# A convolution with per-image mixed weights on one core: the first image pair's five input transfers on two DMA queues, and small products moved around them

## The chip, the core and the metric

The kernel runs on one core of one Trainium2 chip. A core has five engines with instruction streams of their own: TensorE (PE, matrix products into PSUM), VectorE (DVE), ScalarE (ACT), GpSimd (POOL) and SyncE (SP, here only DMA issues and waits). SyncE and ScalarE each ask for DMA transfers on a hardware queue of their own; the profile calls them q1 and q10. Sixteen DMA engines move the data of both. The metric is the device time in microseconds, 304.93 us as the median of three runs of the kernel before (304.77 to 305.39).

## The reference

For x of shape (32, 64, 56, 56), with K = 4 sets of 3x3 weights:

```python
g = gn(x)                                     # group norm, 32 groups of 2 channels, over 2 x 56 x 56 values
pooled = g.mean(axis=(2, 3))
a = relu(einsum('bc,kc->bk', pooled, fc1_w) + fc1_b)
att = softmax(einsum('bk,jk->bj', a, fc2_w) + fc2_b, axis=1)
agg_w = einsum('bk,koihw->boihw', att, weight)     # weights of 64 x 64 x 3 x 3 for each image
agg_b = att @ bias
out = x + conv(g, agg_w, padding=1) + agg_b
```

So an image's convolution can't start before its whole input has been read: the statistics give the attention, the attention mixes the four weight sets, and the mixed weights are what TensorE multiplies with.

## The kernel before

Two images make a pair: 16 pairs, with image and channel on the 128 partitions (2 x 64) and 3136 pixels along a row. All is float32 in memory. For the products, inputs and weights are scaled and split in a high and a low float16 part (xh, xl and wh, wl), and each output tile sums three kinds of product: high by high, high inputs by low weights, low inputs by high weights. Each kind has nine taps, on two 64 x 64 halves of the array. This is the line L1063, 6912 recorded products, in the function `products`.

The order of each engine's instructions is written out by hand, one function for each engine, and semaphores tie them together. Pairs 1 to 15 are prepared while TensorE works on the pair before. Pair 0 has nothing to hide behind, and all that this change touches is its preparation, in this order:

- SyncE (L313 to L323) asks for x0 in four pieces (`PIECES`, in chunks of 448 pixels: 0-2, 2-4, 4-5, 5-7), each with a semaphore `x_piece`. When piece 0 has landed it asks for the first two weight sets, when the last piece has landed for the other two, and when the first half of the weights is there for pair 1's four quarters.
- ScalarE (L916) asks for `small`, the tensor with the attention's weights and biases, then loads its table. It sums chunk 2 of x0 by itself (`sum_chunk`, L882), and after the statistics squares the first two weight sets (`squares`, L874).
- VectorE (`first_stats`, L443) takes the statistics of the other six chunks of 448 pixels, then aggregates them (L472 to L495), forms the logits (L552 to L556) and in `first_mixture` (L631 to L642) the diagonals of the attention and the first third of the mixed weights.
- GpSimd works on b1_part from `small` (L380), then on the moments of chunk 2 (L401 to L410), then the two roots rstd and wnorms (L414, L417), and eye_exsum (L421).
- TensorE runs constant products on ones (`keep_warm`, L1043; their numbers are `WARM_PRODUCTS`), whose results nobody reads, between the small products that it is needed for: the sums (L1010), the range of values (`first_range`, L1016 to L1021), and `part_sum` (L1031, L1037), two shares of the mixed weights. Its first convolution product waits for wh, which ScalarE makes (L863) from VectorE's mix (L642).

Of the kernel before, what the change touches and what calls it, by code (L numbers as in the profile page):

```python
# [28 lines left out]
CHUNK = 448  # L29
CHUNKS = PIX // CHUNK  # L30

PIECES = ((0, 2), (2, 4), (4, 5), (5, 7))
PIECE_OF = (0, 0, 1, 1, 2, 3, 3)

GATE = 0

# [18 lines left out]
TURNED = (2, 3, 0, 1)  # L55

X_RING = 4
WARM_PRODUCTS = (38, 8, 12, 6, 3, 3)

EARLY = 4  # L60

# [48 lines left out]
def dynamic_conv(nc, x, w_t, small, out):  # L110
# [7 lines left out]
    with ctx:  # L118
# [6 lines left out]
        def sem(name):  # L125
            return ctx.enter_context(nc.semaphore(name))
# [86 lines left out]
        s_eye = sem("s_eye")  # L213
        s_diagonal = sem("s_diagonal")
        s_exsum = sem("s_exsum")
        s_eye_exsum = sem("s_eye_exsum")
        s_part_sum = sem("s_part_sum")
        s_const = sem("s_const")
# [57 lines left out]
        def lower_rows(p, m, g, groups=1):  # L276
# [2 lines left out]
            rows *= groups  # L279
            return out_d[p][halves[m], row * W:(row + rows) * W], o_sb[p % 2][1][halves[1 - m], at:at + rows * W]  # L280

        block = ctx.enter_context(nc.Block())

        @block.sync
        def _(sp):
            def load_quarter(p, n):
                if p >= X_RING:

                    for half in range(2):
                        sp.wait_ge(s_xl[half], p - X_RING + 1)  # L290
                pixels = slice(n * HALF // 2, (n + 1) * HALF // 2)
                sp.dma_start(x_sb[p % X_RING][:, pixels], x_d[p, :, pixels]).then_inc(x_in[p % X_RING][n % 2], 16)

            def quarter_landed(p, n):

                sp.wait_ge(x_in[p % X_RING][n % 2], 32 * (p // X_RING - (p % X_RING == 0)) + 16 * (n // 2 + 1))

            def cross_params(p):
                i = p % 2
                sp.wait_ge(s_par, p + 1)  # L300
                for m in range(2):
                    sp.dma_start(crossed[i][halves[1 - m], :], par[i][halves[m], :]).then_inc(s_outp[i], 16)

            def store_groups(p, g, groups=1):

                i, n = p % 2, GROUPS * p + g + groups - 1
                sp.wait_ge(s_res, 2 * n + 1)
                sp.dma_start(*upper_rows(p, g, groups)).then_inc(stored[i][0], 16)
                sp.wait_ge(s_res, 2 * n + 2)
                for m in range(2):  # L310
                    sp.dma_start(*lower_rows(p, m, g, groups)).then_inc(stored[i][1], 16)

            for n, (first, end) in enumerate(PIECES):  # L313
                pixels = slice(first * CHUNK, end * CHUNK)
                sp.dma_start(x_sb[0][:, pixels], x_d[0, :, pixels]).then_inc(x_piece[n], 16)  # L315

            for n, (piece, ks) in enumerate(((GATE, slice(0, 2)), (len(PIECES) - 1, slice(2, K)))):
                sp.wait_ge(x_piece[piece], 16)
                sp.dma_start(w_sb[:, ks, :], w_t[:, ks, :]).then_inc(s_weights[n], 16)
            sp.wait_ge(s_weights[0], 16)  # L320
            for n in range(4):
                load_quarter(1, n)
            cross_params(0)  # L323

            for p in range(2, X_RING):
                for n in range(4):
                    if n >= 2:
                        quarter_landed(p, n - 2)
                    else:
                        quarter_landed(p - 1, n + 2)  # L330
                    load_quarter(p, n)
            for p in range(GROUPED):

                store_groups(p, 0, SLOTS)
                cross_params(p + 1)
                load_quarter(p + X_RING, 0)
                store_groups(p, SLOTS)
                for n in range(1, 4):
                    if n >= 2:
                        quarter_landed(p + X_RING, n - 2)  # L340
                    load_quarter(p + X_RING, n)
            for p in range(GROUPED, PAIRS):

                for g in range(GROUPS if p < last_pair else GROUPS - 1):
                    store_groups(p, g)
                    if g == 2 and p < last_pair:
                        cross_params(p + 1)
                    if p + X_RING < PAIRS:
                        load_quarter(p + X_RING, g)
            i, g = last_pair % 2, GROUPS - 1  # L350
            sp.wait_ge(s_res, 2 * GROUPS * PAIRS - 1)
            sp.dma_start(*upper_rows(last_pair, g)).then_inc(stored[i][0], 16)
            sp.wait_ge(s_res_last, 1)
            sp.dma_start(*lower_rows(last_pair, 0, g)).then_inc(stored[i][1], 16)
            for i in range(2):
                for r in range(2):
                    sp.wait_ge(stored[i][r], 16 * (1 + r) * transfers(PAIRS + i))
# [68 lines left out]
        def _(dve):  # L426
# [146 lines left out]
            def first_scale_step(k):  # L573

                if k == 0:
                    dve.wait_ge(s_exsum, 1)
                    nc.vector.reciprocal(rsum[:], exsum[:]).then_inc(dch, 1)
                    dve.wait_ge(s_range, 3)
                    nc.vector.reciprocal(rtotal[:], total).then_inc(dch, 1)
                elif k == 1:  # L580
                    dve.wait_ge(dch, 4)
# [42 lines left out]
            def first_mixture():  # L624

                dve.wait_ge(s_exp, 1)
                part = PARTS[0]
                dve.wait_ge(s_const, 3)

                for k in range(SUMMED_SHARES):  # L630
                    nc.vector.tensor_scalar(diagonals[:, k, :], eye[:], ex[:, k:k + 1], None, ALU.mult).then_inc(s_diagonal, 1)  # L631
                nc.vector.tensor_reduce(exsum[:], ex[:], AX.X, ALU.add).then_inc(s_exsum, 1)
                dve.wait_ge(s_weights[1], 16)
                nc.vector.tensor_scalar(part_mix[:], w_sb[:, 2, part], ex[:, 2:3], None, ALU.mult).then_inc(s_part, 1)
                first_scale_step(0)
# [44 lines left out]

            def weights_bound():

                dve.wait_ge(s_range, 3)
                nc.vector.tensor_scalar(wbound[:], tiny[1][:, WEIGHTS:WEIGHTS + 1], 1.0 / C, None,
                                        ALU.mult).then_inc(s_bound, 1)

            def low_weights(p):
# [107 lines left out]
        def _(act):  # L795
# [101 lines left out]
            def results(p, g, regions=range(2)):  # L897
                i, n = p % 2, GROUPS * p + g
                for r in regions:
                    if g == 0:  # L900
# [7 lines left out]
                        if p >= 2:  # L908
# [4 lines left out]
                    nc.scalar.activation(o_sb[i][r][:, at:at + rows * W], acc[n % SLOTS][r][:, 0:rows * W], ACT.Identity,  # L913
                                         bias=scales[:, 1:2], scale=scales[:, 0:1]).then_inc(s_res, 1)

            act.dma_start(small_sb[:], small).then_inc(s_small, 16)  # L916
            act.wait_ge(s_warm, 1)
            nc.scalar.activation(warm[:], warm[:], ACT.Exp)
# [78 lines left out]
        def _(pe):  # L997
# [14 lines left out]

            def first_range():

                pe.wait_ge(s_wnorms, 1)
                nc.tensor.matmul(tiny[1][:, WEIGHTS:WEIGHTS + 1], scale[:], wnorms[:],  # L1016
                                 start=True, stop=True).then_inc(s_range, 1)
                nc.tensor.matmul(tiny[1][:, RANGE:RANGE + 1], scale[:], wnorms[:], start=True, stop=False)
                pe.wait_ge(s_first_std, 1)
                for m in range(2):  # L1020
                    nc.tensor.matmul(tiny[1][halves[m], RANGE:RANGE + 1], ones[halves[m], 0:C], std[0][halves[m], :],  # L1021
                                     start=False, stop=True).then_inc(s_range, 1)

            def part_sum():

# [70 lines left out]
            first_range()  # L1096
            keep_warm(3)
            part_sum()
            keep_warm(4)

            pe.wait_ge(s_part, 2)
# [126 lines left out]
```

## Time and profile before

| | |
|---|---|
| median of 3 runs | 304.93 us (304.77 to 305.39) |
| profiled execution, its own time | 304.70 us |
| its span | 302.9 us |
| TensorE busy | 297.3 us (98%) |
| VectorE, ScalarE, GpSimd busy | 246.0, 189.8, 17.7 us |
| chain of waits, share of TensorE | 95% |
| first convolution product | 14.26 us |
| granted TensorE clock | 0.998 |

The span runs from the first to the last recorded instruction; the execution's own time is longer. Times in the rows are microseconds from the span's start. In the chain of waits each piece is what the next one waited for, so only a change in a piece of the chain, or one that puts something else in its place, moves the end.

### The profile page before, as it was taken

Reading aid. Unit: us, or ns where it says so; the run is one execution under the profiler, and the core shown is the slowest. Engines: PE = TensorE matmul, PEld = TensorE weight load, DVE = VectorE, ACT = ScalarE, POOL = GpSimd, SP = SyncE. Lnnn points to the kernel's source line nnn. Section 1 sums busy time; section 2 is a strip of 40 time slices with the busy share of each in tenths; the row PEclk is TensorE's granted clock in tenths of the full one; section 3 lists DMA queues with packets and bytes.
Section 4 is the critical chain, followed back from the end, with each engine's and each line's share of the span. In section 5 each row is a group of like instructions: output and inputs, shape, how many; then the busy total and the mean of one; then the engine's idle time right before and its main releaser. Section 6 shows DMA issues by size and latency. Waiting matters only on the chain.

```text
span 302.9 us, 15877 instructions
## 1 busy us (share of the span) xinstructions
PE 297.3 (98%) x7066; PEld 273.2 (90%) x7066; DVE 246.0 (81%) x799; ACT 189.8 (63%) x246; POOL 17.7 (6%) x30
## 2 busy tenths in 40 slices
PE   8899999999999999999999999999999999999995
PEld 6678997799978997799999999999999999999874
DVE  3898998989999999998998989699696978956000
ACT  3766739194683927385496869567685866768222
POOL 2221040402100000000000000000000000000000
PEclk9999999999999999999999999999999999999999
DMA  7957875737547575846808898685758342332333
GB/s 266 307 166 191 284 231 161 218 131 197 161 150 224 161 208 173 225 157 170 239 26 236 243 232 276 155 257 164 209 135 235 96 122 70 111 101 80 95 112 104
DMA packets 26868, 53.62 MB, mean 177 GB/s; under 512 B 6064, under 2 KB 16432, under 8 KB 26800
## 3 DMA queue, kind: packets, MB, share of 16 engines
q1 hardware_dynamic: 26576, 52.53, 58.6%
q8 instruction: 55, 0.90, 1.3%
q14 instruction: 13, 0.11, 0.1%
q10 hardware_dynamic: 224, 0.07, 0.1%
HBM read 26.89 MB, written 25.69 MB: 174 GB/s over the span
## 4 chain that ended last, share of the span: by engine, by line
PE 95%; DMA 2%; DVE 1%; SPq 0%; issue 0%; POOL 0%; ACT 0%; DVEq 0%
PE acc L1063 94%; DMA x<-x 2%; SPq L315 0%; DVE stats L443 0%; PE tiny L1004 0%; PE acc L1031 0%; PE acc L1043 0%; POOL rstd L414 0%; DVE mv L478 0%; DVE o L791 0%; ACT wh L863 0%; PE tiny L1016 0%; DVE mix L642 0%; PE tiny L1010 0%; DVE sums L490 0%
## 5 line engine op out<-in xcount | busy, mean ns | idle before, releaser
L1063 PE MATMUL acc<-xh,wh 64*64 64x385 f16 (+5 forms) x2304 | 112.6, 325 | 0.3 <-ACT wh L863 0.3
L1063 PE MATMUL acc<-xh,wl 64*64 64x385 f16 (+5 forms) x2304 | 112.4, 325 | 0.0
L1063 PE MATMUL acc<-xl,wh 64*64 64x385 f16 (+5 forms) x2304 | 111.7, 325 | 0.0
L1063 PEld LDWEIGHTS acc<-xl,wh 64*64 64x64 f16 x2304 | 91.4, 107 | 5.9
L1063 PEld LDWEIGHTS acc<-xh,wl 64*64 64x64 f16 x2304 | 90.6, 107 | 6.7
L1063 PEld LDWEIGHTS acc<-xh,wh 64*64 64x64 f16 x2304 | 89.6, 107 | 7.4 <-ACT wh L863 0.5
L913 ACT ACTIVATE o<-acc,par 128x392 f32<-128x392 f32 (+1 forms) x64 | 43.0, 672 | 56.8 <-PE acc L1063 56.8
L457 DVE BATCH_NORM_STATS2 stats<-x 128x6 f32<-128x448 f32 x105 | 61.2, 618 | 1.9
L834 ACT ACTIVATE xh<-x,xof,xsc 128x1568 f16<-128x1568 f32 x24 | 40.5, 1692 | 25.2 <-DVE xof L544 24.7
L701 DVE TENSOR_TENSOR xl<-x,xh 128x1568 f16<-128x1568 f32 x28 | 49.8, 1783 | 3.4 <-ACT x L801 3.2
L592 DVE SCALAR_TENSOR_TENSOR mix<-w_sb,ex,mix 128x576 f32<-128x576 f32 (+1 forms) x69 | 42.9, 621 | 0.5
L913 ACT ACTIVATE o<-acc,crossed 128x392 f32<-128x392 f32 (+1 forms) x63 | 42.4, 673 | 0.5 <-DMA crossed<-par 0.5
L801 ACT ACTIVATE x<-x,xof,xsc 128x1568 f32<-128x1568 f32 x20 | 33.8, 1688 | 0.0
L791 DVE TENSOR_SCALAR o<-acc,crossed 128x224 f32<-128x224 f32 x1 | 0.5, 510 | 19.4 <-PE acc L1063 19.4
L394 POOL TENSOR_TENSOR xl<-x,xh 128x840 f16<-128x840 f32 (+1 forms) x8 | 13.2, 1678 | 50.8 <-DVE xl L701 50.8
L552 DVE SCALAR_TENSOR_TENSOR prod<-tiny,small_sb 128x20 f32<-128x20 f32 x16 | 2.8, 178 | 15.8 <-PE tiny L1004 15.5
L847 ACT ACTIVATE wh<-mix,wsc 128x576 f16<-128x576 f32 (+2 forms) x13 | 9.5, 739 | 7.7 <-DVE mix L599 7.7
L692 DVE SCALAR_TENSOR_TENSOR wl<-mix,wsc,wh 128x576 f16<-128x576 f32 x15 | 12.1, 806 | 1.1 <-ACT wh L847 1.1
L895 ACT ACTIVATE ex<-logit,nmax 128x4 f32<-128x4 f32 x16 | 4.7, 295 | 11.6 <-DVE nmax L556 11.3
L1043 PE MATMUL acc<-ones 128*128 128x256 f16 x70 | 10.2, 307 | 1.5 <-POOL eye L372 1.4
L590 DVE TENSOR_SCALAR mix<-w_sb,ex 128x576 f32<-128x576 f32 (+1 forms) x22 | 9.3, 421 | 2.5 <-ACT ex L895 2.4
L1043 PEld LDWEIGHTS acc<-ones 128*128 128x128 f16 x70 | 7.3, 110 | 3.6 <-POOL eye L372 1.3
(106 smaller groups left out, 161.8 us busy)
## 6 DMA issues: line engine op xcount, KB each, us to landing
x<-x SPq DMA_DIRECT2D x60, 392.0 KB, 4.1
out<-o SPq DMA_DIRECT2D x36, 196.0 KB, 3.8
out<-o SPq DMA_DIRECT2D x72, 98.0 KB, 2.8
out<-o SPq DMA_DIRECT2D x8, 588.0 KB, 3.7
out<-o SPq DMA_DIRECT2D x16, 294.0 KB, 4.3
x<-x SPq DMA_DIRECT2D x3, 448.0 KB, 4.5
w_sb<-w_t SPq DMA_DIRECT2D x2, 576.0 KB, 3.9
out<-o SPq DMA_DIRECT2D x7, 112.0 KB, 2.2
```

Source lines behind the costliest of these rows:

```text
L394: nc.gpsimd.tensor_tensor(xl[i][:, start:end], x_sb[p][:, start:end], xh[i][:, start:end], ALU.subtract).then_inc(done, 1)
L457: ins = nc.vector.bn_stats(stats[:, 0, 6 * t:6 * t + 6], x_sb[p % X_RING][:, t * CHUNK:(t + 1) * CHUNK])
L590: ins = nc.vector.tensor_scalar(**columns, scalar1=ex[:, 0:1], scalar2=None, op0=ALU.mult)
L592: ins = nc.vector.scalar_tensor_tensor(**columns, scalar=ex[:, k:k + 1], in1=mix[:, part], op0=ALU.mult, op1=ALU.add)
L692: nc.vector.scalar_tensor_tensor(out=wl[i][:], in0=mix[:], scalar=wsc[i][:], in1=wh[i][:], op0=ALU.mult, op1=ALU.subtract).then_inc(s_wl, 1)
L701: nc.vector.tensor_tensor(rows_of(xl[i], half), rows_of(x_sb[p % X_RING], half), rows_of(xh[i], half), ALU.subtract).then_inc(s_xl[half], 1)
L801: nc.scalar.activation(v, v, ACT.Identity, bias=xof[i][:], scale=xsc[i][:]).then_inc(s_xn[half], 1)
L834: nc.scalar.activation(rows_of(xh[i], half), rows_of(x_sb[p % X_RING], half), ACT.Identity, bias=xof[i][:], scale=xsc[i][:]).then_inc(s_xh ...
L847: nc.scalar.activation(high[:, rows], mixed_w[:, rows], ACT.Copy, scale=wsc[i][:]).then_inc(s_wh, 1)
L913: nc.scalar.activation(o_sb[i][r][:, at:at + rows * W], acc[n % SLOTS][r][:, 0:rows * W], ACT.Identity, bias=scales[:, 1:2], scale=scales[ ...
L1043: nc.tensor.matmul(acc[SLOTS - 1][0][:, 0:2 * P], ones[:].bitcast(fp16)[:, 0:P], ones[:].bitcast(fp16), start=True, stop=True)
L1063: ins = nc.tensor.matmul(pixels[:, top:bottom, left:right], weights[i][halves[m], tap * C:(tap + 1) * C], window, start=start and step == ...
```

## The change

x0 comes in five pieces in place of four, since the last one is cut in two. SyncE asks for pieces 0, 2 and 4 and ScalarE for pieces 1 and 3, ahead of `small`. The first weights still wait for piece 0, the others for the last piece, which is now number 4. On TensorE the numbers of constant products change from 38, 8, 12, 6, 3, 3 to 38, 6, 15, 4, 3, 3; in `first_range` the two products on std come ahead of the one on wnorms; and the product that gives the weights' bound is moved behind `part_sum`, into another PSUM tile with a semaphore of its own. On VectorE exsum is taken ahead of the two diagonals.

```diff
-PIECES = ((0, 2), (2, 4), (4, 5), (5, 7))
-PIECE_OF = (0, 0, 1, 1, 2, 3, 3)
+PIECES = ((0, 2), (2, 4), (4, 5), (5, 6), (6, 7))
+PIECE_OF = (0, 0, 1, 1, 2, 3, 4)
...
-WARM_PRODUCTS = (38, 8, 12, 6, 3, 3)
+WARM_PRODUCTS = (38, 6, 15, 4, 3, 3)
...
+        def first_piece(n):
+
+            pixels = slice(PIECES[n][0] * CHUNK, PIECES[n][1] * CHUNK)
+            return x_sb[0][:, pixels], x_d[0, :, pixels]
...
-            for n, (first, end) in enumerate(PIECES):
-                pixels = slice(first * CHUNK, end * CHUNK)
-                sp.dma_start(x_sb[0][:, pixels], x_d[0, :, pixels]).then_inc(x_piece[n], 16)
+            for n in range(0, len(PIECES), 2):
+                sp.dma_start(*first_piece(n)).then_inc(x_piece[n], 16)
...
-                    dve.wait_ge(s_range, 3)
+                    dve.wait_ge(s_range, 1)
...
+                nc.vector.tensor_reduce(exsum[:], ex[:], AX.X, ALU.add).then_inc(s_exsum, 1)
 
                 for k in range(SUMMED_SHARES):
                     nc.vector.tensor_scalar(diagonals[:, k, :], eye[:], ex[:, k:k + 1], None, ALU.mult).then_inc(s_diagonal, 1)
-                nc.vector.tensor_reduce(exsum[:], ex[:], AX.X, ALU.add).then_inc(s_exsum, 1)
...
-                dve.wait_ge(s_range, 3)
-                nc.vector.tensor_scalar(wbound[:], tiny[1][:, WEIGHTS:WEIGHTS + 1], 1.0 / C, None,
+                dve.wait_ge(s_weights_range, 1)
+                nc.vector.tensor_scalar(wbound[:], tiny[0][:, WEIGHTS:WEIGHTS + 1], 1.0 / C, None,
...
+            for n in range(1, len(PIECES), 2):
+                act.dma_start(*first_piece(n)).then_inc(x_piece[n], 16)
             act.dma_start(small_sb[:], small).then_inc(s_small, 16)
...
             def first_range():
 
-                pe.wait_ge(s_wnorms, 1)
-                nc.tensor.matmul(tiny[1][:, WEIGHTS:WEIGHTS + 1], scale[:], wnorms[:],
-                                 start=True, stop=True).then_inc(s_range, 1)
-                nc.tensor.matmul(tiny[1][:, RANGE:RANGE + 1], scale[:], wnorms[:], start=True, stop=False)
+
                 pe.wait_ge(s_first_std, 1)
                 for m in range(2):
                     nc.tensor.matmul(tiny[1][halves[m], RANGE:RANGE + 1], ones[halves[m], 0:C], std[0][halves[m], :],
-                                     start=False, stop=True).then_inc(s_range, 1)
+                                     start=True, stop=False)
+                pe.wait_ge(s_wnorms, 1)
+                nc.tensor.matmul(tiny[1][:, RANGE:RANGE + 1], scale[:], wnorms[:], start=False, stop=True).then_inc(s_range, 1)
+
+            def weights_range():
+
+                nc.tensor.matmul(tiny[0][:, WEIGHTS:WEIGHTS + 1], scale[:], wnorms[:],
+                                 start=True, stop=True).then_inc(s_weights_range, 1)
...
             part_sum()
+            weights_range()
             keep_warm(4)
```

The first instructions of ScalarE before, up to its squares of the weights (x is the input, small_sb the small tensor's place, moments the sums of chunk 2):

```order
L916 DMA small_sb<-small 128x32
L918 ACT_TABLE_LOAD
L918 ACTIVATE warm<-warm 128x1
L882 ACTIVATE o,moments<-x 128x448 x2
L890 ACTIVATE means,own<-stats 128x14
L874 ACTIVATE o,wsquares<-w_sb 128x1152
```

and now:

```order
L922 DMA x<-x 128x896
L922 DMA x<-x 128x448
L923 DMA small_sb<-small 128x32
L925 ACT_TABLE_LOAD
L925 ACTIVATE warm<-warm 128x1
L887 ACTIVATE o,moments<-x 128x448 x2
L895 ACTIVATE means,own<-stats 128x14
L879 ACTIVATE o,wsquares<-w_sb 128x1152
```

The small tensor is the third transfer of this queue, behind 896 and 448 pixels of x0; the rest keeps its order.

TensorE before, from the constant products to the first convolution product (tiny and acc are PSUM tiles, ones the constant, diagonals those of the attention):

```order
L1043 MATMUL acc<-ones 128x256 x58
L1010 MATMUL tiny<-sums,ones 64x5 x2
L1016 MATMUL tiny<-wnorms,scale 128x1
L1018 MATMUL tiny<-wnorms,scale 128x1
L1021 MATMUL tiny<-std,ones 64x1 x2
L1043 MATMUL acc<-ones 128x256 x6
L1031 MATMUL acc<-w_sb,diagonals 64x192 x4
L1037 MATMUL acc<-eye_std,eye_exsum 64x64 x2
L1043 MATMUL acc<-ones 128x256 x6
L1063 MATMUL acc<-xh,wh 64x392 x4
```

and now:

```order
L1054 MATMUL acc<-ones 128x256 x59
L1017 MATMUL tiny<-sums,ones 64x5 x2
L1025 MATMUL tiny<-std,ones 64x1 x2
L1028 MATMUL tiny<-wnorms,scale 128x1
L1054 MATMUL acc<-ones 128x256 x4
L1042 MATMUL acc<-w_sb,diagonals 64x192 x4
L1048 MATMUL acc<-eye_std,eye_exsum 64x64 x2
L1032 MATMUL tiny<-wnorms,scale 128x1
L1054 MATMUL acc<-ones 128x256 x6
L1074 MATMUL acc<-xh,wh 64x392 x4
```

Between the sums and the first product on the diagonals there are one product on wnorms and two constant ones fewer; the product for the weights' bound (now L1032) stands behind part_sum.

## Rows read from the trace of the kernel before

**Rows 1.** The chain of waits in order of time: start us, us, what.

```profile
2.10 5.19 DMA x<-x
...
14.26 13.15 PE acc L1063 x311
...
268.50 31.06 PE acc L1063 x742
```

**Rows 2.** Groups by line, 14.2 to 303 us: busy us, mean ns, idle before.

```profile
L1063 PE MATMUL acc<-xh,wh 64*64 64x385 f16 (+5 forms) x2304 | 112.6, 325 | 0.3 <-ACT wh L863 0.3
```

**Rows 3.** Timeline of VectorE, the statistics: start us, us, what, [idle before].

```profile
4.52 2.31 DVE L443 BATCH_NORM_STATS2 stats<-x 128x6 f32<-128x448 f32 x4 [3.67 <-DMA x<-x]
...
7.32 1.15 DVE L443 BATCH_NORM_STATS2 stats<-x 128x6 f32<-128x448 f32 x2 [0.48 <-DMA x<-x]
```

**Rows 4.** Timeline of GpSimd, 4.7 to 7.9 us.

```profile
4.76 0.23 POOL L380 TENSOR_SCALAR b_part<-small_sb 128x4 f32<-128x4 f32 x1 [2.60 <-DMA small_sb<-small]
6.60 0.27 POOL L401 TENSOR_SCALAR moment_square<-moments 128x1 f32<-128x1 f32 x1 [1.61 <-ACT o L882]
...
7.61 0.27 POOL L410 TENSOR_SCALAR stats<-moments,moment_square 128x2 f32<-128x2 f32 x1 [0.17 <-POOL moment_square L407]
```

**Rows 5.** Issue to landing: small tensor, the two of L319, pair 1's quarters.

```profile
small_sb<-small ACTq DMA_DIRECT2D x1, 16.0 KB, 4.0
...
DMA to landing us min/median/max: 3.7/3.9/4.2
...
x<-x SPq DMA_DIRECT2D x4, 392.0 KB, 5.6
```

**Rows 6.** Timeline of SyncE's queue: x0, weights, pair 1.

```profile
0.72 1.81 SPq L315 DMA_DIRECT2D x<-x  x4
4.51 3.13 SPq L319 DMA_DIRECT2D w_sb<-w_t  x2
8.72 1.75 SPq L292 DMA_DIRECT2D x<-x  x4
```

**Rows 7.** Two windows: stretch, length, busy by engine, then PEclk, DMA share, GB/s.

```profile
2.00:3.40 1.40, 1.40 (x8) 1.02 (x7) 0.00 (x0) 0.66 (x2) 0.16 (x1) 1.00 0.62 190
3.40:6.80 3.40, 3.40 (x27) 2.77 (x25) 2.28 (x4) 1.16 (x3) 0.43 (x2) 1.00 1.05 404
```

**Rows 8.** DMA queues, 2.8 to 4.0 us: packets, MB, share of 16 engines.

```profile
q1 hardware_dynamic: 131, 0.42, 88.4%
q10 hardware_dynamic: 128, 0.01, 8.4%
```

**Rows 9.** Timeline of TensorE, 10.4 to 13 us.

```profile
10.42 0.28 PE L1010 MATMUL tiny<-sums,ones 64*64 64x5 f32 x4 [0.41 <-DVE sums L490]
10.72 0.38 PE L1016 MATMUL tiny<-wnorms,scale 128*128 128x1 f32 x2
10.96 0.36 PE L1018 MATMUL tiny<-wnorms,scale 128*128 128x1 f32 x2
...
11.46 0.83 PE L1043 MATMUL acc<-ones 128*128 128x256 f16 x6
12.22 0.87 PE L1031 MATMUL acc<-w_sb,diagonals 64*64 64x192 f32 x8
12.92 0.32 PE L1037 MATMUL acc<-eye_std,eye_exsum 64*64 64x64 f32 x4
```

**Rows 10.** Timeline of all engines, 8.7 to 12.2 us.

```profile
8.79 1.15 ACT L874 ACTIVATE o<-w_sb 128x1152 f32<-128x1152 f32 x1
...
10.11 0.55 POOL L417 TENSOR_TENSOR wnorms<-wsquares,half_power 128x1 f32<-128x1 f32 x1
...
11.72 0.42 DVE L631 TENSOR_SCALAR diagonals<-eye,ex 128x64 f32<-128x64 f32 x2
12.05 0.15 DVE L632 TENSOR_REDUCE exsum<-ex 128x1 f32<-128x4 f32 x1
```

**Rows 11.** Line L457, 14 to 30 us: durations ns, first and last start us.

```profile
L457 DVE BATCH_NORM_STATS2 stats<-x x8: 608/614/627, 18.3 to 26.9; 128x6 f32<-128x448 f32 x8
```

More of the change, by code:

```diff
@@ L215, in dynamic_conv @@
         s_exsum = sem("s_exsum")
+        s_weights_range = sem("s_weights_range")
         s_eye_exsum = sem("s_eye_exsum")
```

## The prediction

> **What bounds the kernel now.** I first read the chain of waits and looked for the engine that carries the end. From 14.26 us to 299.6 us it is one unbroken run of TensorE's convolution products, and the only idle time before them is 0.3 us at their start [rows 1, 2]. So the time is the start of the convolution, plus 285 us of products that this change leaves alone, plus a tail. Whatever moves the start at 14.26 us moves the end by as much, and nothing else in the diff can. The profiled execution took 304.70 us with a span of 302.9, so 1.8 us lie around the span; the median of the three runs is 304.93, 0.23 above it. I add the change to 304.70 and then carry the 0.23 over.
>
> Before 14.26 the chain is this: x0's four transfers land, the last at 2.10 + 5.19 = 7.29 us [rows 1]; VectorE takes their statistics, four chunks from 4.52 to 6.83 and, after an idle 0.48, two from 7.32 to 8.47 [rows 3]; then comes a serial string of small operations through GpSimd, TensorE, VectorE and ScalarE. VectorE's six chunks need 2.31 + 1.15 = 3.46 us of its time, so their end is bound from two sides: 3.46 after the first piece, and one chunk after the last. Only 0.48 of slack lies between the two. GpSimd has its own branch: it waits for the small tensor (4.76), then for the moments (6.60), and is done at 7.61 + 0.27 = 7.88, which is 0.6 before it is needed [rows 4].
>
> **Part 1: the five transfers.** Before, one queue asks for all of x0, first come first served. SyncE issues from 0.72 for 1.81 us [rows 6]. Bytes: from 2.0 to 3.4 the engines move 190 GB/s, 266 KB (thousands of bytes); from 3.4 to 6.8 they move 404 GB/s [rows 7]. The first piece is 459 KB, and by about 3.9 us it and the small tensor's 16 are moved; it is taken up at 4.52, so a landing is seen about 0.59 after the last byte. All of x0 and the small tensor, 1,622 KB, is moved at 3.4 + (1622 - 266)/404 = 6.76, seen at 7.29, 0.53 later. The weights were asked for at 4.51 behind all of x0 on the same queue and take nothing from it. So x0's end is set by bytes, not by issue: a second queue adds no rate there.
>
> How two queues share is shown by the small tensor. Its 16 KB sit on the second queue, asked for at 0.72 like the first piece, and still took 4.0 us to land [rows 5]. Between 2.8 and 4.0 us the engines took 131 packets of queue 1 and 128 of queue 10: one for one [rows 8]. I read this as strict alternation. After the change the first two pieces (459 KB each, same packet size) are on different queues at the same moment, so both end when 917 KB are moved: 3.4 + (917 - 266)/404 = 5.01, plus 0.56 = 5.57, against 4.52 before for the first. The first piece gets later, because the second takes every other packet.
>
> What the second queue can give back is the slow ramp: 266 KB in 1.4 us where 404 GB/s would be 566, a shortfall of 300 KB or 0.74 us.  The bounds are 0 and 0.74 of gain. I take 0.15, near the low end, because the first piece alone, one packet for each of 128 partitions, was there to be taken and the engines still ran slowly; and because the four issues stand only 1.81/4 = 0.45 apart. The first two pieces then land at 5.42. VectorE is bound by its own 3.46: statistics end at 8.88, against 8.47. **Term 1: +0.41 us.** The upper bound is +0.56, with no gain. The lower is -0.30: even if every landing came 0.74 earlier and the first piece were alone, GpSimd's branch (part 2) would end at 8.17. The finer last pieces, which would help if the last landing were the bound, find VectorE behind and are worth nothing; without that cover (VectorE free at the last landing) they would save one chunk, 0.6.
>
> The Trainium skill says in "DMA: Bandwidth & Descriptors", section "Issuing engines are not separate DMA queues", that issuing from several engines only saves the sequencer's time and that the transfers interleave. By that rule alone x0's end would move by no more than the issue time. It agrees with the byte count above, and it says nothing of the first piece, on which this sum turns.
>
> **Part 2: the small tensor,** now third on ScalarE's queue, behind 688 KB. It alternates with the last piece, so it is moved at about 6.76 - 0.15 = 6.61 and seen at 7.15. GpSimd waits for it ahead of the moments: 0.04 to start, 0.23 for b1_part, 0.05, then the 1.28 that lies between 6.60 and 7.88 [rows 4] gives 8.75. That hides 0.13 under the statistics. ScalarE's two more issues, some 0.45 each if like SyncE's [rows 6], stand before its table load and end long before the second piece lands, so they cost nothing.
>
> **Part 3: the weights.** The first half is asked for when piece 0 has landed, so at 5.45 in place of 4.51. The two halves took 3.7 and 4.2 us [rows 5]. This one has no queue in front of it by the time its first bytes can move, so I take 3.7: it lands at 9.15; before, SyncE saw it at 8.72 [rows 6]. ScalarE squares it at once: from the start of the squares at 8.79 to that of the root on GpSimd at 10.11 are 1.32 us, the root takes 0.55 [rows 10], and TensorE's first product on wnorms came 0.06 after it, at 10.72 [rows 9]. So that product can start 1.93 after the landing, at 11.08. TensorE then has one such product (0.26) and four warm products (0.127 each, six filling 11.46 to 12.22 [rows 9]) before part_sum: landing + 2.69 = 11.84. That is hidden, since part_sum waits for the diagonals until 12.53 (below). The cover ends at a landing of 9.84. The second half still waits for x0's last piece and queues behind the first, its bytes end as before; image pair 1 is needed from 18.3 [rows 11] and has about 8 us.
>
> **Part 4: order on TensorE and VectorE.** Before, TensorE did two wnorms products, two for std and six warm ones after the sums, and reached part_sum at 12.22 although the first diagonal was ready at 11.72 + 0.25 = 11.97 [rows 9, 10]. Now one wnorms product (0.24) and two warm products (0.25) are gone from this stretch; TensorE would be free at 11.73, shifted by term 1, and waits for the diagonal instead. exsum now stands ahead of it and delays it by the pitch of such an instruction, 0.07: 12.04, plus 0.07 to TensorE, 12.11 in place of 12.22. **Term 2: -0.11 us.** Bounds: +0.07 if TensorE was not the limit, -0.25 if the diagonal is seen faster and the end of part_sum also stops waiting for eye_exsum; the products of part_sum run 12.22 to 12.92 back to back, so I see little such wait. The weights_range product moves behind part_sum, where TensorE waits for the mix and has room. Of the warm products, the 6 behind x0's landing at 7.14 end near 7.9 (6 times 0.127) and TensorE then idles about 1 us until the statistics; 15 products then fill 1.9 us, as long as the sums take (8.47 to 10.42), so they delay nothing. The granted clock is 1.00 in all these windows [rows 7], with gaps of 0.4 us; I price a 1 us gap at nothing, at most at some tenths if the start of the convolution ran at half rate.
>
> **Sum.** +0.41 - 0.11 = +0.30 us. Start of the convolution 14.56, own time 305.00, on the median's scale 305.23.
>
> **Rivals.**
> Late weights (slower). If the first half lands at L later than 9.84, TensorE's wnorms product holds part_sum: start = L + 2.69, a change of L - 9.53 us. ScalarE is held as much, since squares stand ahead of the exponential. For: the first weights took 4.2 (L = 9.65), and the four quarters issued from 8.72 took 5.6 in the middle [rows 5], which would give L = 11.05. Against: those had a full queue ahead. At L = 10.35 it is +0.8, 305.5 own, 305.8; at 11.05, +1.5.
> No alternation (same side, smaller). If each engine drained its share of a whole transfer before turning to the other queue, the first piece would keep 4.52, VectorE would end near 7.9, and the small tensor, last of its queue, would set the end: 7.25 + 1.60 = 8.85, +0.38 - 0.11 = +0.27, 305.20. The 131 against 128 packets speak against it. The Trainium skill, same page, section "Queues, rings and completion order", has the engines switch only after some 9 to 17 descriptors, which would be about one engine's share here; the trace disagrees with it.
> The ramp vanishes (faster). With the whole 0.74: pieces at 4.83, statistics at 8.29, GpSimd at 8.16, so -0.18 - 0.11 = -0.29, own time 304.41, 304.64. For: 190 GB/s. Against: one queue was enough to reach 404.
> It does not do what it says. If ScalarE's ring starts so much later that the first piece is alone as before, the small tensor still comes late: between -0.1 and +0.2, 304.9 to 305.1.
>
> **Chances.** Forecast 0.52, late weights 0.15, no alternation 0.12, ramp gone 0.10, no effect 0.05, unforeseen 0.06. Range: 304.5 takes in the ramp case and the noise of the median, 305.9 half of the late weights. A measurement tells 0.2%, 0.6 us, from no change: faster by that is more than any case here gives (0.10, for what I don't see and the edge of the ramp case), slower comes from the late weights and the forecast's upper tail (0.20), the rest, 0.70, is within.
>
> **What would show it.** First statistics chunk at about 5.4 and no later gap among the six; statistics' end near 8.9; small tensor seen near 7.1; squares starting near 9.2; part_sum 0.1 earlier relative to the statistics' end; first convolution product near 14.6, and from there an unchanged run. I am wrong if the first chunk starts before 5.0 or the first two pieces land far apart, if squares start after 9.9, or if the convolution's 285 us change.

## The result, and the profile after

The changed kernel took 306.72 us as the median of nine runs (305.47 to 307.25), against 304.93 before (304.74 to 305.39): 1.0039 times the time of before, interval 1.0024 to 1.0053, so slower by 1.2 us (0.7 to 1.6). The two medians lie 1.8 apart, since the middle one of the nine falls in the upper of two groups. I had said 305.2, within 304.5 and 305.9. The groups are four from 305.47 to 305.81 and five from 306.72 to 307.25. Two causes are mixed in this median: a start of the convolution that is late in every execution, and something more that comes in only a part of them. In a second set the same kernel had a median of 305.63 (12 runs), with eight of them up to 305.72, against 305.10 before: ratio 1.0016 (0.9998 to 1.0034), which doesn't exclude no change. How much the change costs at the median thus depends on how many runs fall in the upper group; the late start is in both profiled executions.

The profiled execution belongs to the first group: 305.51 us, 0.81 over the profiled one of before. Its chain of waits (start us, us, what):

```profile
0.72 4.85 DMA x<-x
...
5.59 4.65 DMA w_sb<-w_t
...
10.26 1.26 ACT o L879 x2
...
11.59 0.56 POOL wnorms L422
...
12.20 0.38 PE tiny L1028 x2
...
13.04 0.80 PE acc L1042 x8
...
15.00 13.15 PE acc L1074 x312
...
269.23 31.06 PE acc L1074 x742
```

Against [rows 1] the convolution starts at 15.00 in place of 14.26. Behind that nothing changed: its last step begins 0.73 later than before and is as long. And the chain no longer goes through x0's last piece and the statistics. It goes from the first piece to the first weights, which take 4.65 us to land, to their squares, to the root on GpSimd and to the product on wnorms.

The timelines of VectorE and GpSimd in the same execution, where before had [rows 3] and [rows 4]:

```profile
5.60 3.26 DVE L448 BATCH_NORM_STATS2 stats<-x 128x6 f32<-128x448 f32 x6 [4.75 <-DMA x<-x]
9.39 0.01 DVE L477 LOAD_MASK_SELECT stats<-stats  x1 [0.54 <-POOL stats L415]
```
```profile
7.76 0.23 POOL L385 TENSOR_SCALAR b_part<-small_sb 128x4 f32<-128x4 f32 x1 [5.61 <-DMA small_sb<-small]
...
9.09 0.27 POOL L415 TENSOR_SCALAR stats<-moments,moment_square 128x2 f32<-128x2 f32 x1 [0.17 <-POOL moment_square L412]
```

The six chunks run without a gap from 5.60 to 8.86, so VectorE is bound by its own work, as forecast. But it then stands still for 0.54 us, waiting for GpSimd, whose work on the moments had to wait for the small tensor until 7.76. Here is the second late arrival, and it reaches TensorE at nearly the same time as the first: the first diagonal is ready at 12.83 (started at 12.58, 0.25 long), the constant products behind the late wnorms product end at 12.97, when part_sum begins (12.22 in [rows 9]).

Windows of this execution (stretch, length, busy by engine, then clock, DMA share, GB/s), beside [rows 7]:

```profile
2.00:3.40 1.40, 1.40 (x8) 0.99 (x7) 0.00 (x0) 1.26 (x1) 0.15 (x1) 1.00 0.72 182
3.40:6.80 3.40, 3.40 (x18) 2.35 (x16) 1.20 (x3) 1.23 (x5) 0.00 (x0) 1.00 1.03 387
6.80:7.30 0.50, 0.50 (x5) 0.35 (x4) 0.50 (x2) 0.40 (x2) 0.00 (x0) 1.00 0.91 143
7.30:8.60 1.30, 1.30 (x14) 1.17 (x13) 1.30 (x3) 0.00 (x0) 0.74 (x3) 1.00 0.74 237
```

Two queues move no more than one: 182 GB/s in the ramp and 387 behind it, against 190 and 404. From 6.8 to 7.3 the engines are busy 0.91 of their time and move 143 GB/s, and the weights come at 237. It is not the small tensor that takes the time. The two queues in 6.8 to 7.3 (packets, MB, share of the 16 engines' time), q1 with the weights and the end of x0, q10 with the small tensor alone:

```profile
q1 hardware_dynamic: 26, 0.07, 84.0%
q10 hardware_dynamic: 44, 0.00, 6.8%
```

And q1 from 7.2 to 7.8, when only weights move, in this execution and then in the one of before:

```profile
q1 hardware_dynamic: 19, 0.09, 69.4%
```
```profile
q1 hardware_dynamic: 54, 0.25, 100.1%
```

The same packets of the weights, some 4.6 KB each, take 0.35 us of an engine here (0.694 x 16 x 0.6 / 19) and 0.18 before. There the weights were asked for at 4.51, long before x0 was through, and moved at 415 GB/s from 6.8 on; here, asked for at 5.59, their slow first packets are on the path. x0 too had begun slowly (190 GB/s from 2.0 to 3.4, [rows 7]).

### The profile page after: what moved, and what is told of

Same layout as the page of the kernel before. It is cut to its first block, busy times and chain, and to the rows that moved or that the text cites. A ratio compares the mean times of both kernels' runs of the same rounds, so it can differ in the third digit from the quotient of the medians.

```text
span 303.6 us, 15876 instructions
## 1 busy us (share of the span) xinstructions
PE 297.9 (98%) x7065; PEld 273.4 (90%) x7065; DVE 245.9 (81%) x799; ACT 189.6 (62%) x246; POOL 17.8 (6%) x30
## 4 chain that ended last, share of the span: by engine, by line
PE 95%; DMA 3%; ACT 1%; DVE 0%; POOL 0%; issue 0%; DVEq 0%
PE acc L1074 94%; DMA x<-x 2%; DMA w_sb<-w_t 2%; ACT o L879 0%; PE tiny L1011 0%; PE acc L1042 0%; POOL wnorms L422 0%; DVE o L796 0%; ACT wh L868 0%; PE acc L1054 0%; PE tiny L1028 0%; DVE mix L647 0%; PE acc L1048 0%; DVEq L794 0%; DVEq L646 0%
## 5 line engine op out<-in xcount | busy, mean ns | idle before, releaser
L399 POOL TENSOR_TENSOR xl<-x,xh 128x840 f16<-128x840 f32 (+1 forms) x8 | 13.2, 1674 | 51.1 <-DVE xl L706 51.1
L1054 PE MATMUL acc<-ones 128*128 128x256 f16 x69 | 10.8, 328 | 1.3 <-POOL eye L377 1.3
L1054 PEld LDWEIGHTS acc<-ones 128*128 128x128 f16 x69 | 8.0, 119 | 3.6 <-POOL eye L377 1.3
```

The lines of the kernel that those rows point to most:

```text
L399: nc.gpsimd.tensor_tensor(xl[i][:, start:end], x_sb[p][:, start:end], xh[i][:, start:end], ALU.subtract).then_inc(done, 1)
L1054: nc.tensor.matmul(acc[SLOTS - 1][0][:, 0:2 * P], ones[:].bitcast(fp16)[:, 0:P], ones[:].bitcast(fp16), start=True, stop=True)
```

## The experiments

Theory A says that two late arrivals, the small tensor and the first weights, each hold the start by about 0.7 us, side by side. Rival B says that the statistics' delay is the loss, as I had forecast it. Theory C says that the group near 307 has TensorE at its lower clock at the start of the convolution. Times of before in these sets had medians of 304.94 to 305.10.

**The small tensor first on its queue** (small_first).

```diff
+            act.dma_start(small_sb[:], small).then_inc(s_small, 16)
             for n in range(1, len(PIECES), 2):
                 act.dma_start(*first_piece(n)).then_inc(x_piece[n], 16)
-            act.dma_start(small_sb[:], small).then_inc(s_small, 16)
```

> The changed kernel with one line moved: ScalarE asks for the small tensor before pieces 1 and 3. Theory A (two late arrivals hold the start of the convolution side by side: the small tensor through GpSimd, and the first weights through the squares and the product on wnorms): the statistics' shuffle goes back from 9.39 to about 9.0 us, but the weights still land near 10.2, so part_sum stays at about 12.95 and the first convolution product at 14.95 to 15.0; the time stays that of the changed kernel (profiled 305.5). Rival B (VectorE's later statistics, as forecast, are the whole loss, the weights are hidden): with the small tensor out of the way the first product comes at about 14.6, profiled 305.1. Theory C (the runs near 307 come from TensorE falling to its lower clock at the start of the convolution): such runs appear here too, since TensorE's idle stretches stay.

Measured: 305.00 us (304.83 to 305.68, 12 runs), ratio to before 0.9992 (0.9971 to 1.0013), first convolution product at 14.41. All three expectations missed, since the edit moved more than I thought, and so it doesn't tell the theories apart. Its timeline:

```profile
4.48 1.15 DVE L448 BATCH_NORM_STATS2 stats<-x 128x6 f32<-128x448 f32 x2 [3.63 <-DMA x<-x]
...
6.27 2.43 DVE L448 BATCH_NORM_STATS2 stats<-x 128x6 f32<-128x448 f32 x4 [0.63 <-DMA x<-x]
...
8.79 1.75 SPq L298 DMA_DIRECT2D x<-x  x4
```

The first piece is back at 4.48 and the first weights, which wait for it, are seen at 8.79. This is the alternation of [rows 8] at work: the small tensor's packets stand ahead of piece 1 in the second queue and take its turns, at 128 bytes each, while piece 0 goes through. So one line moved gave back 0.59 us of the start (15.00 to 14.41).

**The first weights without their wait** (weights_early).

```diff
-                sp.wait_ge(x_piece[piece], 16)
+                if n == 1:
+                    sp.wait_ge(x_piece[piece], 16)
```

> The changed kernel, with the first two weight sets asked for at once behind x0's pieces, without a wait for piece 0. Theory A: the weights land near 8.8 in place of 10.24, squares no longer hold anything, but the small tensor still lands at 7.7 and GpSimd ends its moments at 9.36; part_sum then starts when the diagonal is there, 12.9 in place of 12.97: first product at about 14.9, 0.05 to 0.1 earlier. Rival B: the same as theory A or a little better; rival D (the weights alone are the loss): first product near 14.3. Theory C: the runs near 307 become rarer if the 0.47 us idle before the wnorms product is what lowers the clock.

Measured: 306.10 us (305.78 to 308.96, 12 runs), ratio 1.0039 (1.0013 to 1.0065), first product at 15.35, profiled 305.88. The weights came at 8.88, as expected, but the small tensor was later still:

```profile
8.14 0.23 POOL L386 TENSOR_SCALAR b_part<-small_sb 128x4 f32<-128x4 f32 x1 [5.98 <-DMA small_sb<-small]
```

Now its packets share with the weights' behind x0: from 7.0 to 7.5 the engines took 48 packets of q1 and still 12 of the small tensor's. So with one late arrival gone the other alone holds the start, and by more: 15.35 is 1.13 past one_queue4 below. That one arrival suffices agrees with theory A; the number of theory A was wrong by 0.45, as I had kept the small tensor's landing fixed.

**Transfers as before, the rest of the change kept** (one_queue4).

```diff
-PIECES = ((0, 2), (2, 4), (4, 5), (5, 6), (6, 7))
-PIECE_OF = (0, 0, 1, 1, 2, 3, 4)
+PIECES = ((0, 2), (2, 4), (4, 5), (5, 7))
+PIECE_OF = (0, 0, 1, 1, 2, 3, 3)
...
-            for n in range(0, len(PIECES), 2):
+            for n in range(len(PIECES)):
                 sp.dma_start(*first_piece(n)).then_inc(x_piece[n], 16)
...
-            for n in range(1, len(PIECES), 2):
-                act.dma_start(*first_piece(n)).then_inc(x_piece[n], 16)
```

> The changed kernel with the transfers as before: four pieces on SyncE's queue, only the small tensor on ScalarE's. All the rest of the change stays (38, 6, 15, 4 constant products, order of wnorms and std, exsum first). All theories: statistics end at 8.48, small tensor at 4.7, weights at 8.7; part_sum waits only for the diagonal, 12.11 in place of 12.22, so the first product is at 14.15 and the profiled time 304.6, 0.1 under the kernel before. Theory C with the numbers of products as its cause: runs about 1.7 us longer appear here too, since 6 in place of 8 products leave TensorE idle 0.2 us more; with the late arrivals as its cause: none appear.

Measured: 304.84 us (304.70 to 305.34, 12 runs), ratio 0.9981 (0.9961 to 1.0001), first product at 14.22, clock 0.998 or more in all. The whole loss of the change lies in the transfers. The new order of small products is worth 0.04 us in the start, not the 0.11 of term 2: part_sum again starts at 12.22. A difference as small as that is read from one execution of each kernel and could be theirs. No run at a lower clock appears in the twelve, so the changed numbers of constant products don't by themselves bring such runs.

**The transfers alone** (queues_only: the kernel before, with the pieces and both queues of the changed one).

> The kernel before with the five pieces on two queues alone; TensorE and VectorE keep their old order and 38, 8, 12, 6 products. Theory A: weights at 10.24, so the first wnorms product starts at 12.20 and the two for wnorms, the std ones (0.74 together) and six constant ones (0.76) stand between it and part_sum: 13.70, first product at about 15.7, profiled 306.2, 1.5 over the kernel before. Rival B: part_sum at 12.22 + 0.4, first product 14.7, 305.1. So the rest of the change is worth 0.7 under theory A and 0.1 under B. Theory C: some runs 1.7 us above the rest, as in the changed kernel.

Measured: 307.10 us (306.22 to 309.19, 12 runs), ratio 1.0067 (1.0040 to 1.0093), the profiled one 306.22, first product at 15.77, part_sum at 13.75. Theory A is met within 0.1 and B is out by 1.1. The same reordering that is worth 0.04 with weights in time is worth 15.77 - 15.00 = 0.77 with late ones, since it takes products out from between wnorms and part_sum.

**Each late arrival by itself, on one queue.** In small_late SyncE asks for the small tensor behind x0; in weights_late the first weights wait for x0's last piece. Both start from one_queue4.

```diff
+            sp.dma_start(small_sb[:], small).then_inc(s_small, 16)
...
-            act.dma_start(small_sb[:], small).then_inc(s_small, 16)
```
```diff
-GATE = 0
+GATE = 3
```

> One queue with four pieces as in one_queue4, but the small tensor is asked for last, by SyncE behind x0. This isolates one of the two late arrivals. It lands with x0's end, about 7.35. Theory A: GpSimd does b1_part at 7.39 and ends the moments 1.60 later, 8.99, so the shuffle goes from 8.65 to 9.02 and the first product from 14.22 to 14.6, +0.37. Rival F (GpSimd's order doesn't matter, only VectorE's last chunk does): 14.2.

> One queue with four pieces as in one_queue4, but the first weights wait for x0's last piece, like the second. This isolates the other late arrival. They are asked for at 7.33 and take 3.7, so they land at 11.0. Theory A: the product on wnorms starts 1.93 later at 12.95, part_sum 2.7 after the landing at 13.7 in place of 12.22, and the first product at 15.7; profiled 306.2. Theory B: 14.2, 304.7. Theory C: with an idle TensorE from 11 to 12.9 some runs lie another 1.7 us higher.

small_late: 305.76 us (305.33 to 307.26, 10 runs), ratio 1.0028 (1.0012 to 1.0044). Its profiled execution falls to the lower clock at 13.5, so I compare what comes before. The small tensor is taken up at 7.76, 0.4 later than I expected, the shuffle follows at 9.40 and part_sum at 12.96: +0.74 over 12.22, twice the expected 0.37 because of that landing, and as much as the changed kernel loses. weights_late: 307.78 us (307.75 to 307.92, 4 runs), ratio 1.0089 (1.0074 to 1.0104). The weights are there at 11.11, the wnorms product starts at 13.04, 1.93 later, and part_sum at 13.82, 2.71 after them; the first product came at 16.40, not 15.7, and most of the difference is the clock (below). So the small tensor alone costs what the changed kernel loses, and the weights, by the same 2.7 behind a landing at 10.24, would too: theory A. That second half is worked out, since no run has the weights land at 10.24 with the small tensor on time. F is out.

**Both late arrivals taken out, the late statistics left in** (statistics_alone: weights_early, and the small tensor asked for by SyncE between pieces 0 and 2).

> The changed kernel with both late arrivals taken out and the late statistics left in: pieces 0 and 1 still start together on the two queues, but the small tensor is asked for by SyncE right behind piece 0, and the first weights without a wait, behind x0 on the same queue. Theory A with the forecast's first term under it: the first piece is seen at about 5.6, the statistics end at 8.86 as in the changed kernel, the small tensor is seen before 7.3 and the weights near 9. What is left is the statistics' delay: first product at 14.22 + 0.35 = 14.6, profiled 305.1, fastest runs 305.0 to 305.2. Rival B', that the statistics' delay counts only through the small tensor: 14.2. Theory C: no or few runs at a lower clock, since TensorE idles little between 10.8 and 12.4.

Measured: 305.16 us (304.99 to 305.46, 11 runs), ratio 1.0005 (0.9996 to 1.0014), clock 0.999 or more in all.

```profile
5.83 3.26 DVE L451 BATCH_NORM_STATS2 stats<-x 128x6 f32<-128x448 f32 x6 [4.98 <-DMA x<-x]
...
9.21 0.01 DVE L480 LOAD_MASK_SELECT stats<-stats  x1
...
14.80 1.19 PE L1076 MATMUL acc<-xh,wh 64*64 64x392 f16 x24
```

VectorE is now held by nothing but its own chunks. Their end is 9.09, 0.59 past one_queue4's, and the first product 0.58 past its 14.22. The forecast's first term is real and passes to the start one for one; it was hidden under the other two. The first piece was 0.2 later than expected, and so was all behind it. This rests on the trace: the times alone, 0.22 over the median of before at a ratio whose interval holds 1, wouldn't show it.

**The clock.** In after_again the changed kernel ran once more, filled has more constant products (38, 10, 18, 4 and four before the wait for wnorms), bare only the first 38.

```diff
-WARM_PRODUCTS = (38, 6, 15, 4, 3, 3)
+WARM_PRODUCTS = (38, 10, 18, 4, 3, 3, 4)
...
+                keep_warm(6)
                 pe.wait_ge(s_wnorms, 1)
```
```diff
-WARM_PRODUCTS = (38, 6, 15, 4, 3, 3)
+WARM_PRODUCTS = (38, 0, 0, 0, 0, 0)
```

> The changed kernel once more, for the comparison within this set. Theory C (two things add up: the first convolution product 0.74 us later, and in part of the executions a spell of TensorE at its lower clock at the start of the convolution, worth about 1.7 us): the fastest runs at 305.5, some third to half of them between 306.7 and 307.3, with a granted clock of 0.993 or 0.994 in most of these.

> The changed kernel with 38, 10, 18, 4 constant products in place of 38, 6, 15, 4, and four more between the products on std and the wait for wnorms. No arrival moves, so the first product stays at 15.0 and the fastest runs at 305.5 under every theory. Theory C: with less idle on TensorE the runs near 307 become rare, one in ten or fewer, and the median falls to about 305.6. Rival E (the runs near 307 are noise of the transfers, late data in some executions): they stay as frequent as in the changed kernel.

> The changed kernel with only the first 38 constant products; those behind x0's landing, behind the statistics, before and behind part_sum and before the convolution are left out. Theory C: TensorE idles for most of 7.5 to 15 us, so the convolution starts at the lower clock in nearly every run; products of the first stretch take about twice as long in the profile, and all runs lie 1.5 us or more above 305.5. Rival E: 305.4 to 305.6 in most runs, since nothing waits for a constant product.

after_again: 305.63 us (305.25 to 307.31, 12 runs), ratio 1.0016 (0.9998 to 1.0034), two of twelve at the lower clock and not the third to half that I expected; its profiled execution took 306.76 and is one of the two. It shows what such a run near 307 is. Windows around the first product, then TensorE's timeline:

```profile
12.80:13.20 0.40, 0.40 (x6) 0.33 (x6) 0.40 (x4) 0.40 (x2) 0.24 (x1) 0.99 0.98 361
13.20:16.60 3.40, 3.40 (x28) 2.26 (x27) 2.38 (x12) 2.29 (x5) 0.00 (x0) 0.50 0.89 327
16.60:17.00 0.40, 0.40 (x16) 0.22 (x8) 0.30 (x2) 0.40 (x1) 0.00 (x0) 0.99 0.20 78
```
```profile
10.94 0.28 PE L1017 MATMUL tiny<-sums,ones 64*64 64x5 f32 x4 [0.44 <-DVE sums L495]
11.19 0.28 PE L1025 MATMUL tiny<-std,ones 64*64 64x1 f32 x4
12.08 0.38 PE L1028 MATMUL tiny<-wnorms,scale 128*128 128x1 f32 x2 [0.61 <-POOL wnorms L422]
...
14.70 1.44 PE L1054 MATMUL acc<-ones 128*128 128x256 f16 x6
16.07 0.93 PE L1074 MATMUL acc<-xh,wh 64*64 64x392 f16 x12
```

From 13.2 to 16.6 the granted clock is 0.50, the lower of TensorE's two levels (1.2 in place of 2.4 GHz). Before it fell TensorE had gone from 10.5 to 12.3 with little but idling and products of a few columns. The first profile has such a stretch too, from 10.8 to 12.4, and kept its clock, so such a stretch makes a spell possible and not certain. The six constant products ahead of the convolution take 1.44 us in place of 0.81, and the first product waits for them: 16.07, where the first profile had 15.00. VectorE's last operation comes at 301.70 in place of 300.38, although part_sum had begun 0.12 earlier (12.85 for 12.97), so the spell costs 1.4 us. weights_late idles for longer (nothing on TensorE from 12 to 13) and shows the spell in all its four runs:

```profile
12.00:13.00 1.00, 0.00 (x0) 0.00 (x0) 0.00 (x0) 1.00 (x4) 0.56 (x2) 1.00 0.84 160
13.00:14.00 1.00, 0.95 (x8) 0.72 (x10) 0.81 (x7) 1.00 (x3) 0.84 (x2) 1.00 1.01 392
14.00:15.00 1.00, 1.00 (x14) 0.84 (x13) 0.48 (x4) 0.69 (x1) 0.00 (x0) 0.96 1.07 389
15.00:16.00 1.00, 1.00 (x6) 0.73 (x7) 0.96 (x5) 0.67 (x2) 0.00 (x0) 0.50 0.97 361
```

Runs with a mean clock of 0.994 or less:

| kernel | such runs | their times, us | the others start at |
|---|---|---|---|
| before, all sets | 5 of 102 | 306.9 to 308.0 | 304.67 |
| one_queue4, one_queue5, small_first, statistics_alone | 0 of 47 | | 304.15 |
| changed (both sets) | 5 of 21 | 306.8 to 307.3 | 305.25 |
| weights_early | 3 of 12 | 307.4 to 309.0 | 305.78 |
| small_late | 3 of 10 | 306.9 to 307.3 | 305.33 |
| queues_only | 6 of 12 | 307.2 to 309.2 | 306.22 |
| weights_late | 4 of 4 | 307.8 to 307.9 | |
| bare | 6 of 6 | 308.4 to 312.1 | |
| filled | 0 of 12 | | 305.27 |

For nine of the 102 runs of before no clock is on record; their longest took 305.39.

bare, at 308.93 us (ratio 1.0128, 1.0089 to 1.0166), meets theory C. filled is at 305.82 us (305.27 to 306.98, 12 runs; 1.0019, 1.0003 to 1.0035): no spell in twelve, against 5 in 21, points the same way but is too little to show it, and the median did not fall to 305.6. Four of its runs lie between 305.96 and 306.98 at full clock. Two of the changed kernel's first nine (306.72 and 307.21) are long at full clock too, and five of before lie between 305.93 and 306.58 in the same way. I have no trace of such a run: what they are stays open.

**Five pieces on one queue** (one_queue5: one_queue4 with the changed kernel's five pieces).

> The changed kernel with the five pieces all on SyncE's queue in order and the small tensor alone on ScalarE's. Arrivals as before, but the last landing holds one chunk of 448 pixels and not two: chunk 5 is taken when VectorE is free at 6.83, chunk 6 at about 7.35, statistics end at 7.97 in place of 8.48. Then the string behind them moves up 0.5 us, unless the weights, at 8.72, hold it: landing + 2.69 = 11.4 for part_sum against 11.7 for the diagonals, so they don't. First product at 13.75, profiled 304.2, 0.5 under the kernel before. Rival: ScalarE's squares can't start before 8.75 and push the exponential, which cuts the gain to 0.2 or 0.3; GpSimd's moments end at 7.88 and allow it.

Measured: 304.40 us (304.15 to 305.31, 12 runs), ratio to before 0.9974 (0.9959 to 0.9990). It beats both kernels. From its profile (304.18 us):

```profile
4.53 3.52 DVE L448 BATCH_NORM_STATS2 stats<-x 128x6 f32<-128x448 f32 x6 [3.68 <-DMA x<-x]
...
8.16 0.01 DVE L477 LOAD_MASK_SELECT stats<-stats  x1
```

The first product is at 13.76, as expected. Here the finer last piece pays, because VectorE starts at 4.53 and is free when it lands: the two bounds that [rows 3] left 0.48 apart now meet.

## Why the prediction was wrong

What held. The convolution's run is untouched: from the first product to VectorE's last operation 285.38 us, against 285.40. The pieces alternate and the first is late: 5.59 for 5.42. The statistics end at 8.86 for 8.88, by two errors that cancel: the piece is 0.17 later, and six chunks back to back take 3.26, not 3.46. The second queue adds no rate, which is the rule of the Trainium skill that I had weighed ("DMA: Bandwidth & Descriptors", section "Issuing engines are not separate DMA queues"); by the traces the gain of 0.15 that I took from the ramp was nothing. That page's rule on whole packets of descriptors (section "Queues, rings and completion order") is contradicted again: both first pieces landed 4.9 to 5.0 us after their issue.

What failed, in order of weight.

Part 3, "so I take 3.7: it lands at 9.15". The first weights took 4.65 and landed at 10.24. The step after it was right: "landing + 2.69" gives 12.93 for part_sum and it began at 12.97, and the rival's L - 9.53 gives +0.71 for a measured +0.74. I gave that rival 0.15 although the rows had 3.7, 4.2 and 5.6 for such transfers, and I took the shortest; the middle one of the three, 4.2, would have left only 0.2 of cover. The reason I gave, no queue in front, points the wrong way. A new transfer starts slowly: x0 did in [rows 7], the weights did here at 0.35 us a packet, and in weights_late, with nothing else moving from 6.8 to 8.0, they did again (134 GB/s from 8.2 to 9.2, then 424 from 9.5). A queue in front had hidden that start; asked for 1.08 us later, they showed it. I had the row of the slow start and used it for x0 alone. It isn't the whole of it: weights_late needed 3.8 us from issue to landing, 0.8 less, while here the weights stayed near 240 GB/s up to 10.2, and why they did is open.

Part 2, "seen at 7.15", hidden by 0.13. It was taken up at 7.76, and GpSimd ended at 9.36, 0.50 past the statistics. Three parts of about 0.2 each make up the miss: the 0.15 of the ramp that wasn't gained; x0's last piece, for which SyncE waits before it asks for the other weights, at 7.52 in place of 7.31; and the small tensor, taken up 0.24 after that where I had them together. In small_late, on a single queue, the two times are 7.51 and 7.76. It wasn't for want of engine time: there 64 of the 110 packets from 6.8 to 7.3 were under 512 bytes, and the engines moved 429 GB/s. What delays the small landing behind x0's isn't shown. A cover of 0.13 on a landing known to some 0.5 was no cover.

Part 4, "I price a 1 us gap at nothing". It was not the gap that I meant, behind x0's landing. Nor did [rows 7], whose windows end at 6.80, say anything of the clock there. The late arrivals opened another stretch, from 10.5 to 12.3, and the low-clock spells came in 5 of 21 runs against 5 of 102. The counts are small: within the set of after_again they are 2 of 12 against 3 of 29. It needn't be the wnorms product that is late: in small_late it followed at once on the products on std, what had grown was the idle time ahead of the sums (0.65), and 3 of 10 runs had the spell. Spells are worth 1.4 us when they come; three of the nine timed runs have them, and with the two unexplained ones they set the median.

Term 2, -0.11, was -0.04: with exsum ahead, the diagonal is ready at 12.08 and TensorE takes 0.14 to begin, where I had 0.07.

All four errors have one sign, so the forecast's upper tail was too thin. And the size of the miss is in part the draw of the nine runs: the second set's median of 305.63 lies within what I had said, although the weights and the small tensor came late there too (taken up at 10.14 and 7.50).

## What to carry to other kernels

Here two queues shared packet by packet, so the second one didn't bring bytes sooner; it made the first transfer later and let what stood last on a queue, however small, wait for nearly everything: put tiny tensors that something waits for at the head of a queue. A transfer that something waits for is best asked for while the queue ahead of it is still full, so that its slow start is hidden. In weights_early that made the small tensor later still, so the small ones come first. When several arrivals feed one start, work out each as if it were alone and give it the spread of the landings in the trace: a branch hidden by less than that spread is not hidden. And a wait on TensorE ahead of its long run had a second price here, the lower clock in part of the executions, so look at the spread of runs and not only at the one profile.

## What the runs showed of the hardware

- A tensor of 16 KB in rows of 128 bytes took little of the engines' time (44 packets, a share of 0.068 for half a microsecond). At the head of its own queue it cost the first piece nothing (4.48), and landed 3.9 us after its issue, against 6.0 as third.
- The first half of the weights, 576 KB, took 3.8 us from issue to landing in weights_late and 4.65 to 4.9 in the profiles of the changed kernel and of filled. Asked for at 4.51, it moved at 415 GB/s from 6.8 to 7.3 (before); asked for at 5.59, the engines moved 143 GB/s in the same half microsecond (changed). weights_late shows the slow start with nothing else moving.
- The constant products took 0.42 us each up to 3.9 us and 0.27 from 4.7 us (before), while the profile gives a granted clock of 1.00 for both, as in [rows 7]: its first microseconds can't be read as full clock.
- The clock's spell lasted 3.4 us at 0.50 in after_again and was gone by 16.6 although TensorE had not been idle since 12.3; in bare it lasted from about 13.7 to 20.5. The kernel before has it too, in 5 of 102 runs.
